# Normalising and storing the output rows inside the experts' block, with the rows of the later experts corrected afterwards

## The chip, the cores and the metric

The kernel runs on one core of one Trainium2 chip. The metric is the device time of one execution in microseconds (us), the median over several executions. Lower is better.

## What is computed

A decoder layer on 4 x 2048 tokens of 256 float32 values: attention with a layer norm, then a mixture of experts with a second layer norm. Only the second part is touched.

```python
logits = relu(x @ rw1 + rb1) @ rw2 + rb2
vals, ids = top_k(logits, 2)                     # two experts of eight for each token
probs = softmax(vals)
disp[e, pos] = x of the tokens sent to expert e  # at most 1024 rows for each expert
eo = relu(disp @ ew1 + eb1) @ ew2 + eb2
y = eo[ids, pos] * probs, summed over the two experts
out = layernorm(x + y)                           # over the 256 values of a row
```

So a row of the output needs the token's own x, the row of its first and the row of its second expert. Rows of one expert lie anywhere in the batch.

## The kernel before

The program has blocks with a barrier between them: projections, attention, `mix_and_route`, `experts`, `normalize`. `mix_and_route` writes x to the DRAM table `z_rows` and scatters every row, with three tags behind its 256 values (row number, rank, gap of the two logits), into `dispatched`.

**experts.** The rows of the 8 experts are worked in 16 halves of 512 rows (4 tiles of 128), named 0 to 15 here. Half 10 and 11 are those of expert 5, half 14 and 15 those of expert 7, the last. For each half TensorE (PE) runs `first` (8 groups of 6 matmuls, one group for each 128 of the 1024 hidden values), turns the next half's rows, and runs `second` (96 matmuls). Every product is made of three, with operands split into a high and a low float32r part. ScalarE (ACT) makes two ReLU copies of each group (L1867, L1870); VectorE (DVE) subtracts them (L1940) and signals `hid_done`. `first` waits for `hid_done` of the group four places back, since there are four banks; ACT's second copy waits for that of two groups back, since `hid` has two buffers. In even halves ACT and DVE also split the next expert's weights (L1844, L1847, L1887), which ends with the signal `weights_split`. DVE adds the bias (L1921), multiplies by the share (L1929), and GpSimd (POOL) issues four accumulating indirect DMAs for each half (L1776), which add 128 rows each into `z_rows`. After each odd half POOL waits until its adds have landed (`expert_added`). SP loads the rows of later halves, weights and biases.

**normalize.** After the barrier SP loads all of `z_rows` in 16 chunks of 512 rows; DVE makes the statistics and the scale of each row, ACT normalises three tiles of a chunk, POOL the fourth, and SP stores the chunk.

```python
            for ci in range(NCH):
                sp.dma_start(z[:, ci], z_src[ci]).then_inc(z_in[ci], 16)
            for ci in range(NCH):
                sp.wait_ge(act_result, MINE * (ci + 1))
                sp.wait_ge(pool_result, ci + 1)
                sp.dma_start(out_dst[ci], result[:, ci]).then_inc(stored, 16)
```

The order of every queue is written out by hand, in the order of the code.

Of the kernel before, what the change touches and what calls it, by code (L numbers as in the profile page):

```python
# [21 lines left out]
U32 = mybir.dt.uint32  # L22
# [20 lines left out]
TAGS = 3  # L43
ROW = C + TAGS
ROW_ID, FIRST, GAP = C, C + 1, C + 2
# [19 lines left out]
class Carried:  # L65
# [4 lines left out]
    def __init__(self, nc, ctx):  # L70
# [11 lines left out]
        self.rw1_in = s.sem("rw1_in")  # L82
# [726 lines left out]
def attend(nc, a, d, kept, first):  # L809
# [10 lines left out]
    with ExitStack() as ctx:  # L820
# [53 lines left out]
        def _(sp):  # L874
# [31 lines left out]
            def first_rows():  # L906

                for i in range(2):
                    sp.wait_ge(y_out[i], 16 * G * NC // 2)
                load_sums(sp, d, slice(0, EARLY), kept.sums[:], kept.sums_in[0])  # L910
                load_values(sp, d, 0, kept.yk, kept.rows_in[0])
                load_values(sp, d, 1, kept.yk1, kept.rows_in[1])
                sp.dma_start(kept.xr[:], x_src[0]).then_inc(kept.rows_in[0], 16)
                sp.dma_start(kept.rw1[:], a["rw1"].rearrange("(k p) n -> p k n", p=P)).then_inc(kept.rw1_in, 16)
# [141 lines left out]
        def _(pool):  # L1056
# [5 lines left out]
            nc.gpsimd.tensor_copy(empty_rows[:, :, ROW_ID].bitcast(U32), empty_ids[:]).then_inc(empty_set, 1)  # L1062
# [93 lines left out]
def mix_and_route(nc, a, d, kept, early):  # L1156
# [8 lines left out]
    with ExitStack() as ctx:  # L1165
# [20 lines left out]
        row_ids = sb("row_ids", [P, B * NC, TT])  # L1186
# [297 lines left out]
        def _(act):  # L1484
# [33 lines left out]
            ready(act, kept.rw1_in, 16)  # L1518
# [9 lines left out]
        def _(dve):  # L1528
# [84 lines left out]
            def place(c, n):  # L1613
# [18 lines left out]
                v.tensor_copy(tags[:, :, ROW_ID].bitcast(U32), row_ids[:, ci])  # L1632
# [62 lines left out]
def experts(nc, a, d, early):  # L1695


    HALVES = 2 * E
    RING = 4
    with ExitStack() as ctx:  # L1700
# [4 lines left out]
        rows = sb("rows", [P, RING, TT, ROW])  # L1705
        row_ids = sb("row_ids", [P, RING, TT], U32)
        is_first = sb("is_first", [P, RING, TT])
        other = sb("other", [P, RING, TT])
        ratio = sb("ratio", [P, RING, TT])
        total = sb("total", [P, RING, TT])  # L1710
        share = sb("share", [P, RING, TT])
# [10 lines left out]
        eo = sb("eo", [P, 2, TT, C])  # L1722
        xt_ps = [ps(f"xt{i}", [P, CH]) for i in range(KC)]
# [3 lines left out]
        rows_in = [sem(f"rows_in{i}") for i in range(RING)]  # L1727
        turned = sem("turned")
# [10 lines left out]
        expert_added = sem("expert_added")  # L1739
        share_step = sem("share_step")  # L1740
        other_done = sem("other_done")
        ratio_done = sem("ratio_done")
        share_done = sem("share_done")
        added = [sem(f"added{i}") for i in range(2)]
        block = ctx.enter_context(nc.Block())

        rows_src = d["disp"].rearrange("(h t p) c -> h p t c", p=P, t=TT)

        @block.sync
        def _(sp):  # L1750
            def load_rows(q):
                if q >= RING:
                    sp.wait_ge(turned, KC * (q - RING + 1))
                    sp.wait_ge(other_done, q - RING + 1)
                sp.dma_start(rows[:, q % RING], rows_src[q]).then_inc(rows_in[q % RING], 16)

            for q in range(RING):
                load_rows(q)
            for q in range(HALVES):
# [4 lines left out]
                if q + RING < HALVES:  # L1764
                    load_rows(q + RING)
                if q % 2 and e < E:
                    sp.wait_ge(eo_done, 2 * (q + 1))
                    early.load_biases(sp, e, e % SUBS)

        @block.gpsimd  # L1770
        def _(pool):
            for q in range(HALVES):
                pool.wait_ge(eo_weighed, TT * (q + 1))
                pool.sem_inc(early.due, 1)
                for t in range(TT):
                    pool.indirect_dma_start(  # L1776
                        d["z"], bass.IndirectOffsetOnAxis(ap=row_ids[:, q % RING, t:t + 1], axis=0),
                        eo[:, q % 2, t, :], None, compute_op=ALU.add,
                    ).then_inc(added[q % 2], 16)
                if q % 2:  # L1780
                    for i in range(2):
                        pool.wait_ge(added[i], 16 * TT * (q // 2 + 1))
                    pool.sem_inc(expert_added, 1)
# [54 lines left out]
        def _(act):  # L1838
# [16 lines left out]

            high_w1(0)
            rows_of(0)
            high_w2(0)
            for q in range(HALVES):
# [12 lines left out]
                act.wait_ge(other_done, q + 1)  # L1872
                nc.scalar.activation(ratio[:, q % RING], other[:, q % RING], ACT.Exp).then_inc(ratio_done, 1)
                if q + 1 < HALVES:
                    rows_of(q + 1)
                if q % 2 == 0 and q // 2 + 1 < E:
                    high_w1(q // 2 + 1)
                    high_w2(q // 2 + 1)

        @block.vector  # L1880
        def _(dve):
# [14 lines left out]
            def read_tags(q):  # L1896
                at = q % RING
                dve.wait_ge(rows_in[at], 16 * (q // RING + 1))
                if q >= RING:
                    dve.wait_ge(expert_added, q // 2 - 1)  # L1900
                nc.vector.tensor_copy(row_ids[:, at], rows[:, at, :, ROW_ID].bitcast(U32))
                nc.vector.tensor_scalar(is_first[:, at], rows[:, at, :, FIRST], rev[:, q // 2:q // 2 + 1], 2.0,
                                        ALU.is_equal, ALU.mult).then_inc(share_step, 1)
                dve.wait_ge(share_step, 2 * q + 1)
                nc.vector.scalar_tensor_tensor(other[:, at], is_first[:, at], -1.0, rows[:, at, :, GAP],
                                               ALU.add, ALU.mult).then_inc(other_done, 1)

            def weights_of(q):
                at = q % RING
                dve.wait_ge(ratio_done, q + 1)  # L1910
                nc.vector.tensor_scalar(total[:, at], ratio[:, at], 1.0, None, ALU.add).then_inc(share_step, 1)
                dve.wait_ge(share_step, 2 * q + 2)
                nc.vector.reciprocal(share[:, at], total[:, at]).then_inc(share_done, 1)

            def add_bias(q):
# [7 lines left out]
                dve.wait_ge(share_done, q + 1)  # L1923
                if q >= 2:
                    dve.wait_ge(expert_added, q // 2)
# [222 lines left out]
```

## Time and profile before

| | us |
|---|---|
| time, median of 3 executions (2829.73 to 2831.21) | 2830.01 |
| time of the profiled execution | 2830.7 |
| its span, from the first to the last instruction | 2828.7 |
| start of the experts' block | 2384.7 |
| start of `normalize` | 2781.8 |

The trace is that of one execution. A row of a timeline or of a group names engine, line, operation and the tiles read and written; an idle time in brackets has the instruction that ended it. Names that end in q (SPq, POOLq) are an engine's queue, with the instructions that only issue DMAs, wait or drain.

### The profile page before, as it was taken

The numbers are of one execution on the slowest core, as the hardware profiler recorded it, in microseconds if no ns is written. First come the engines' busy times: TensorE is split into PE (matmuls) and PEld (weight loads), VectorE is DVE, ScalarE is ACT, GpSimd is POOL, SyncE is SP. The second block draws the span as 40 slices with busy tenths as digits, with TensorE's granted clock in tenths as the row PEclk, the third lists the DMA queues.
The fourth block names the chain that finished last, engine by engine and source line by source line (L and its number), as shares of the span: only waits on it lengthen the run. The fifth ranks groups of instructions, "written<-read, shape, count | busy, mean of one in ns | idle before, by whom it ended". The sixth has DMA issues, their size and how long they took to land. (4 is left out here: it accounts for less than half of the span.)

```text
span 2828.7 us, 46886 instructions
## 1 busy us (share of the span) xinstructions
PE 2703.0 (96%) x16154; PEld 1869.5 (66%) x16154; DVE 2092.8 (74%) x5500; ACT 1785.7 (63%) x3322; POOL 760.1 (27%) x721
## 2 busy tenths in 40 slices
PE   8999989999999999999999999999899996999991
PEld 7888855666655656666665666566377774999991
DVE  7888879888888888888888888887355553545444
ACT  5666626677777677766777777777654444655554
POOL 7888820100100110110110010011025553222222
PEclk9999979999999999999999999999999997999995
DMA  6878863233442442532533333431074432343317
GB/s 218 281 266 281 283 171 87 65 99 94 105 106 77 98 98 61 132 83 75 119 82 91 85 91 85 104 91 51 12 222 150 127 105 80 76 103 84 72 23 245
DMA packets 241853, 337.91 MB, mean 119 GB/s; under 512 B 37986, under 2 KB 125195, under 8 KB 240336
## 3 DMA queue, kind: packets, MB, share of 16 engines
q1 hardware_dynamic: 223952, 311.72, 38.7%
q0 software_dynamic: 17664, 23.19, 4.1%
q8 instruction: 129, 2.11, 0.3%
q14 instruction: 108, 0.88, 0.1%
HBM read 191.47 MB, written 152.86 MB: 122 GB/s over the span
## 5 line engine op out<-in xcount | busy, mean ns | idle before, releaser
L1048 ACT ACTIVATE att_probs<-att_score_bank 128x512 f32<-128x512 f32 (+1 forms) x2240 | 1127.3, 596 | 460.6 <-PE att_score_bank L991 450.7
L1095 DVE TENSOR_REDUCE att_partial_max<-att_max_bank 128x1 f32<-128x512 f32 x1536 | 979.6, 682 | 173.0 <-PE att_max_bank L977 171.5
L991 PE MATMUL att_score_bank<-att_q_st,att_k_st 98*128 98x512 f32 (+3 forms) x1792 | 578.9, 381 | 7.8 <-DMA att_q_st<-att_max_rows 6.0
L977 PE MATMUL att_max_bank<-att_k_st,att_q_st 96*128 96x512 f32 (+3 forms) x1792 | 570.8, 374 | 1.7 <-DVE att_partial_max L1095 0.8
L1077 POOL TENSOR_SCALAR_AFFINE_SELECT att_probs<-att_probs 128x512 f32<-128x512 f32 x256 | 162.0, 635 | 1499.1 <-ACT att_probs L1048 1499.0
L1008 PE MATMUL att_acc_bank<-att_probs,att_v_st 128*32 128x512 f32 (+3 forms) x5120 | 528.2, 536 | 0.0
L1101 DVE CUSTOM_DVE_ANT_0 att_edge_sum<-att_max_bank,first_edge 128x256 f32<-128x256 f32 (+3 forms) x1024 | 459.5, 483 | 67.6 <-PE att_max_bank L977 65.6
L991 PEld LDWEIGHTS att_score_bank<-att_q_st,att_k_st 98*128 98x128 f32 x1792 | 319.8, 190 | 163.2 <-ACT att_probs L1048 80.6
L977 PEld LDWEIGHTS att_max_bank<-att_k_st,att_q_st 96*128 96x128 f32 x1792 | 330.2, 190 | 136.3 <-DVE att_partial_max L1095 53.1
L1008 PEld LDWEIGHTS att_acc_bank<-att_probs,att_v_st 128*32 128x32 f32 x5120 | 136.7, 109 | 248.8 <-issue 140.3
L289 POOL TENSOR_TENSOR proj_op_low<-proj_turned,proj_op_high 128x512 fp32r<-128x512 f32 x192 | 244.2, 1297 | 47.3 <-ACT proj_op_high L449 44.7
L1867 ACT ACTIVATE exp_hid_high<-exp_hid_bank,exp_b 128x512 fp32r<-128x512 f32 x128 | 88.3, 690 | 158.1 <-PE exp_hid_bank L1809 147.9
L1776 POOL DMA_INDIRECT z_rows<-exp_eo,exp_row_ids x64 | 108.4, 1694 | 287.6 <-DVE exp_eo L1929 241.7
L977 PE MATMUL att_max_bank<-first_k,att_q_st 96*128 96x512 f32 (+3 forms) x432 | 169.9, 415 | 6.1 <-DMA att_v_st<-v_tokens 5.6
L1509 ACT ACTIVATE mix_hid<-mix_hid_bank,mix_rb 128x512 f32<-128x512 f32 x128 | 87.7, 685 | 136.6 <-PE mix_hid_bank L1428 136.5
L1374 POOL DMA_INDIRECT dispatched<-mix_x,mix_scatter_idx x128 | 129.5, 1011 | 148.0 <-DVE mix_x L1634 112.3
L449 ACT ACTIVATE proj_op_high<-proj_turned 128x512 fp32r<-128x512 f32 x192 | 121.1, 631 | 68.8 <-DVE proj_turned L518 67.1
L1940 DVE TENSOR_TENSOR exp_hid_low<-exp_hid,exp_hid_high 128x512 fp32r<-128x512 f32 x128 | 88.6, 692 | 83.9 <-ACT exp_hid L1870 83.9
L991 PE MATMUL att_score_bank<-att_q_st,first_k 98*128 98x512 f32 (+3 forms) x432 | 150.6, 398 | 0.0
L1826 PE MATMUL exp_eo_bank<-exp_w_high,exp_hid_high 128*128 128x256 f32 x512 | 146.2, 286 | 0.0
L1826 PE MATMUL exp_eo_bank<-exp_w_high,exp_hid_low 128*128 128x256 f32 x512 | 145.0, 283 | 0.0
L1826 PE MATMUL exp_eo_bank<-exp_w_low,exp_hid_high 128*128 128x256 f32 x512 | 145.0, 283 | 0.0
(239 smaller groups left out, 4235.9 us busy)
## 6 DMA issues: line engine op xcount, KB each, us to landing
qk_parts<-proj_parts SPq DMA_DIRECT2D x64, 1024.0 KB, 5.2
att_k_st<-qk_parts SPq DMA_DIRECT2D x168, 256.0 KB, 6.5
att_q_st<-qk_parts SPq DMA_DIRECT2D x159, 256.0 KB, 4.5
v_tokens<-proj_v_tok SPq DMA_DIRECT2D x64, 256.0 KB, 4.6
att_v_st<-v_tokens SPq DMA_DIRECT2D x64, 256.0 KB, 7.2
y_heads<-kept_y_raw SPq DMA_DIRECT2D x64, 256.0 KB, 2.3
exp_w<-in_ew SPq DMA_DIRECT2D x16, 1024.0 KB, 8.7
first_q<-qk_parts SPq DMA_DIRECT2D x33, 256.0 KB, 4.4
```

Source lines behind the costliest of these rows:

```text
L289: nc.gpsimd.tensor_tensor(op_low[:, c % OPS, i], turned[:, c % 2, i], op_high[:, c % OPS, i].bitcast(F32), ALU.subtract).then_inc(lows_don ...
L449: nc.scalar.activation(op_high[:, c % OPS, i], turned[:, c % 2, i], ACT.Copy).then_inc(highs_done, 1)
L977: last = nc.tensor.matmul(max_ps[u % MAXB][:, at:end], q_tile(n)[0:3 * L, head, tile * P:(tile + 1) * P], k_tile(g, kb)[0:3 * L, head, 0:e ...
L991: last = nc.tensor.matmul(score_ps[h % SCOREB][:, i * (CH - q0):(i + 1) * (CH - q0)], k_tile(g, kt // TT)[:, j + i, (kt % TT) * P:(kt % TT ...
L1008: last = nc.tensor.matmul(acc[j * L:(j + 1) * L, q0:CH], v_st[:, g % 2, kt // TT, kt % TT, j * L:(j + 1) * L], probs[:, k % PROBS, j, q0:C ...
L1048: nc.scalar.activation(probs[:, k % PROBS, j:j + heads, q0:CH], score_ps[h % SCOREB][:, 0:heads * (CH - q0)].rearrange("p (j n) -> p j n", ...
L1077: nc.gpsimd.affine_select(out=block_probs, in_=block_probs, pattern=[[0, HG], [1, P]], compare_op=ALU.is_ge, fill=zero, base=0, channel_mu ...
L1095: nc.vector.tensor_reduce(partial_max[:, m % 2, j * TT + t, kb:kb + 1], bank[:], AX.X, ALU.max).then_inc(unit_reduced, 1)
L1101: last = nc.vector.tensor_tensor_reduce(out=edge_sum[:, u % 2, at:end], in0=bank[:, at:end], in1=edge[:, CH - end + at:CH], scale=1.0, sca ...
L1374: pool.indirect_dma_start(d["disp"], bass.IndirectOffsetOnAxis(ap=scatter_idx[:, c[1] % SUBS, kt:kt + 1], axis=0), x1[:, c[1] % ROUND, kt ...
L1776: pool.indirect_dma_start(d["z"], bass.IndirectOffsetOnAxis(ap=row_ids[:, q % RING, t:t + 1], axis=0), eo[:, q % 2, t, :], None, compute_o ...
L1826: last = nc.tensor.matmul(eo_ps[i][:, t, :], x[:, m, part], w[:, sub, m], start=(m == 0 and n == 0), stop=(m == MC - 1 and n == 2))
```

## The change

`normalize` is gone. Its work stands in the queues of `experts`, from half 10 on. It is done on units: c0 to c15 are chunks of 512 output rows, h10 to h15 the rows of one half.

- A chunk is loaded from `z_rows` when the adds of a given half have landed (`half_added`, now signalled after every half), normalised in place by ACT (three tiles) and POOL (one) and stored. c0 to c2 are loaded before half 10 is added, c3 to c5 before half 11, c6 to c8 before half 12, c9 and c10 before half 13, c11 to c15 after it.
- Rows that a later half changes are corrected: POOL gathers them by row number from `z_rows` (`gather`), ACT and DVE normalise two tiles each, and POOL scatters them into the output (`fix`), with a bound that leaves out rows whose chunk had not been stored yet.
- Expert 7's halves 14 and 15 are no longer added to `z_rows`. Their rows are gathered ahead, DVE adds the weighted result to them, and they are normalised and scattered directly.
- The statistics of a chunk or half are made either between the subtractions of half q (STATS_FIRST) or after them, ahead of the bias (STATS_SECOND).
- Every dispatched row has a fourth tag, its row in the output. The tags of all 16 halves are loaded once, by one DMA of 128 x 16 x 4 runs of 16 bytes, and all shares are computed once, in half 0; the DVE and ACT instructions that did it in each half (L1901 to L1913, L1873) are gone. Rows are loaded without tags, into a ring of 3 in place of 4.
- The DMA that loads `rw1` in attention counts on another semaphore, `consts_in`.

```diff
-TAGS = 3
+TAGS = 4
-ROW_ID, FIRST, GAP = C, C + 1, C + 2
+ROW_ID, FIRST, GAP = C, C + 2, C + 3
...
+HALVES = 2 * E
+LAST = HALVES - 2
+LOADED_IN = {10: (0, 1, 2), 11: (3, 4, 5), 12: (6, 7, 8), 13: (9, 10), 14: (11, 12, 13, 14, 15)}
+STATS_FIRST = {11: ("c1", "c2"), 12: ("c5",), 13: ("h10", "h11"), 14: ("c9", "c10"), 15: ("c13", "h12")}
+STATS_SECOND = {10: ("c0",), 11: ("c3", "c4"), 12: ("c6",), 13: ("c7", "c8"), 14: ("c11", "c12"), 15: ("h13", "c14", "c15")}
+def norms_in(q):
+    return STATS_SECOND.get(q - 1, ()) + STATS_FIRST.get(q, ())
...
-    RING = 4
+    RING = 3
+    SPARE = 5
...
 SP queue of experts, for each half q, between the loads of rows and of biases:
+                if q in LOADED_IN:
+                    sp.wait_ge(half_added, q)
+                    if q == 11:
+                        sp.wait_ge(weights_split, 2 * (E - 1))
+                    if q == 13:
+                        sp.wait_ge(weights_split, 2 * E)
+                    if q == LAST:
+                        sp.wait_ge(stored[0], 16 * 6)
+                    for i in LOADED_IN[q]:
+                        load_chunk(i)
...
+                if q > 10:
+                    for u in norms_in(q):
+                        if is_chunk(u):
+                            store_chunk(u)
...
 GpSimd queue of experts:
-            for q in range(HALVES):
-                pool.wait_ge(eo_weighed, TT * (q + 1))
...
+            def gather(q):
+                for t in range(TT):
+                    pool.indirect_dma_start(
+                        unit(f"h{q}")[:, t, :], None, d["z"],
+                        bass.IndirectOffsetOnAxis(ap=ids[:, q, t, 0:1], axis=0)).then_inc(gathered[max(q, 11)], 16)
+
+            def fix(q, group):
+                pool.wait_ge(act_result, results(f"h{q}", TT - 1, 2))
+                pool.wait_ge(dve_result, results(f"h{q}", 0, 2))
                 pool.sem_inc(early.due, 1)
                 for t in range(TT):
                     pool.indirect_dma_start(
-                        d["z"], bass.IndirectOffsetOnAxis(ap=row_ids[:, q % RING, t:t + 1], axis=0),
+                        out_rows, bass.IndirectOffsetOnAxis(ap=ids[:, q, t, 1:2], axis=0),
+                        unit(f"h{q}")[:, t, :], None, bounds_check=bounds[group], oob_is_err=False,
+                    ).then_inc(fixed[group], 16)
+
+            def add(q):
+                pool.wait_ge(eo_weighed, TT * (q + 1))
+                for i in LOADED_IN.get(q, ()):
+                    pool.wait_ge(*loaded_at[i])
+                if q == 12:
+                    pool.wait_ge(gathered[11], 16 * 2 * TT)
...
+                pool.wait_ge(added, 16 * TT * (q + 1))
+                pool.sem_inc(half_added, 1)
+
+            for q in range(LAST - 1):
+                add(q)
+                if q == 11:
+                    pool.wait_ge(weights_split, 2 * E)
+                    gather(10)
+                    gather(11)
+                if q == 12:
+                    pool.wait_ge(stored[0], 16 * 6)
+                    fix(10, 0)
+                    fix(11, 0)
+                for u in norms_in(q + 1):
+                    if q + 1 > 10 and is_chunk(u):
+                        norm_chunk(u)
+            add(LAST - 1)
+            gather(LAST)
+            pool.wait_ge(fixed[0], 16 * 2 * TT)
+            gather(12)
+            for u in norms_in(LAST):
+                if is_chunk(u):
+                    norm_chunk(u)
+            gather(13)
+            gather(LAST + 1)
+            for u in norms_in(HALVES - 1):
+                if is_chunk(u):
+                    norm_chunk(u)
+            pool.wait_ge(stored[1], 16 * 5)
+            fix(12, 1)
+            norm_chunk("c14")
+            norm_chunk("c15")
+            fix(13, 1)
+            pool.wait_ge(stored[2], 16 * 5)
+            pool.wait_ge(fixed[1], 16 * 2 * TT)
+            fix(LAST, 2)
+            fix(LAST + 1, 2)
+            pool.wait_ge(fixed[2], 16 * 2 * TT)
...
 ScalarE queue of experts, after the eight ReLU pairs of half q:
+                if q == 0:
+                    act.wait_ge(share_step, 4)
+                    nc.scalar.activation(ratio[:], other[:], ACT.Exp).then_inc(ratio_done, 1)
+                if q > 10:
+                    for u in norms_in(q):
+                        deviation(u)
                 if q + 1 < HALVES:
                     rows_of(q + 1)
...
+                if q in range(11, HALVES - 1):
+                    for u in sorted(norms_in(q), key=is_chunk):
+                        norm(u)
+            norm("h12")
+            deviation("h13")
+            norm("h13")
+            for u in ("c11", "c12", "c13"):
+                norm(u)
+            for u in ("c14", "c15", "h14", "h15"):
+                deviation(u)
+                norm(u)
...
 VectorE queue of experts:
+            def arrived(u):
+                if is_chunk(u):
+                    dve.wait_ge(*loaded_at[number(u)])
+                elif number(u) < LAST:
+                    dve.wait_ge(gathered[max(number(u), 11)], 16 * TT * (2 if number(u) < 12 else 1))
...
                 for m in range(MC):
                     dve.wait_ge(hid_high_done, MC * q + m + 1)
                     nc.vector.tensor_tensor(hid_low[:, m], hid[:, m % 2], hid_high[:, m].bitcast(F32),
                                             ALU.subtract).then_inc(hid_done, 1)
+                    if m < len(tiles):
+                        stats_of(*tiles[m])
+                        if m:
+                            moments_of(*tiles[m - 1])
...
+            all_moments("h13")
+            all_moments("c14")
+            finish_half("h13")
+            all_moments("c15")
+            scales_of("c14")
+            all_moments("h14")
+            scales_of("c15")
+            finish_half("h14")
+            add_bias(HALVES - 1)
+            all_moments("h15")
+            finish_half("h15")
-def normalize(nc, d, out):
...
```

## Rows read from the trace of the kernel before

**Rows 1.** The page, part 1: engine, busy us (share of the span), instructions.

```profile
PE 2703.0 (96%) x16154; PEld 1869.5 (66%) x16154; DVE 2092.8 (74%) x5500; ACT 1785.7 (63%) x3322; POOL 760.1 (27%) x721
```

**Rows 2.** Stretches: PE, PEld, DVE, ACT, POOL busy, granted clock, DMA share, GB/s.

```profile
2698.30:2721.70 23.40, 23.40 (x154) 21.42 (x154) 9.90 (x23) 11.22 (x20) 6.81 (x4) 1.00 0.20 24
...
2782.00:2828.70 46.70, 0.00 (x0) 0.00 (x0) 29.62 (x160) 30.65 (x65) 8.87 (x16) 0.50 0.98 360
```

**Rows 3.** Timeline 2762 to 2800: start us, us, engine, line, operation, [idle before].

```profile
2765.96 0.69 DVE L1921 TENSOR_TENSOR exp_eo_sum<-exp_eo_bank,exp_b 128x512 f32<-128x512 f32 x1 [5.07 <-PE exp_eo_bank L1826]
...
2774.74 1.55 POOL L1776 DMA_INDIRECT z_rows<-exp_eo,exp_row_ids  x1 [0.31 <-issue]
2781.78 9.43 SPq L1997 DMA_DIRECT2D fin_z<-z_rows  x16
...
2785.04 1.41 DVE L2028 BATCH_NORM_STATS2 fin_stats<-fin_z 128x6 f32<-128x256 f32 x4 [17.35 <-DMA fin_z<-z_rows]
```

**Rows 4.** Issues of the final stores, L2001: ns min/median/max, first and last start.

```profile
L2001 SPq DMA_DIRECT2D out<-fin_result x16: 792/1336/5053, 2791.3 to 2820.7; - x16
```

**Rows 5.** SP and POOL at block ends (L1700 experts', L1959 normalize's).

```profile
L1700 POOLq DRAIN  x1: 2982/2982/2982, 2778.6 to 2778.6; - x1
...
L1959 POOLq DRAIN  x1: 691/691/691, 2815.5 to 2815.5; - x1
```

**Rows 6.** Indirect DMAs by line: ns min/median/max; then issue to landing, us.

```profile
L1374 POOL DMA_INDIRECT dispatched<-mix_x,mix_scatter_idx x128: 978/981/1509, 2097.8 to 2379.3; - x128
...
DMA to landing us min/median/max: 2.1/2.5/5.0
```

**Rows 7.** The same for the accumulating scatters of the experts.

```profile
L1776 POOL DMA_INDIRECT z_rows<-exp_eo,exp_row_ids x64: 1539/1557/2023, 2419.9 to 2774.7; - x64
...
DMA to landing us min/median/max: 3.6/4.1/8.6
```

**Rows 8.** POOL timeline, the first two adds of half 12.

```profile
2699.45 1.55 POOL L1776 DMA_INDIRECT z_rows<-exp_eo,exp_row_ids  x1 [15.58 <-DVE exp_eo L1929]
2701.30 1.79 POOL L1776 DMA_INDIRECT z_rows<-exp_eo,exp_row_ids  x1 [0.30 <-issue]
```

**Rows 9.** ACT timeline, turned rows in half 12, start of half 13.

```profile
2685.80 1.08 ACT L1854 ACTIVATE exp_rows_high<-exp_xt_bank 128x512 fp32r<-128x512 f32 x2
...
2698.32 0.69 ACT L1867 ACTIVATE exp_hid_high<-exp_hid_bank,exp_b 128x512 fp32r<-128x512 f32 x1 [7.84 <-PE exp_hid_bank L1809]
```

**Rows 10.** DVE timeline, halves 12 and 13.

```profile
2685.84 0.69 DVE L1940 TENSOR_TENSOR exp_hid_low<-exp_hid,exp_hid_high 128x512 fp32r<-128x512 f32 x1 [0.67 <-ACT exp_hid L1870]
...
2688.71 4.49 DVE L1887 TENSOR_TENSOR exp_w_low<-exp_w,exp_w_high 128x2048 fp32r<-128x2048 f32 x2 [0.98 <-ACT exp_w_high L1844]
...
2697.54 1.13 DVE L1929 TENSOR_SCALAR exp_eo<-exp_eo_sum,exp_share 128x256 f32<-128x256 f32 x4
```

**Rows 11.** PE timeline: half 12 begins; its second layer begins after the turning.

```profile
2673.43 0.40 PE L1809 MATMUL exp_hid_bank<-exp_rows_high,exp_w_high 128*128 128x512 f32 x1
...
2685.14 0.36 PE L1826 MATMUL exp_eo_bank<-exp_w_high,exp_hid_high 128*128 128x256 f32 x1
```

**Rows 12.** Groups by line from 2350: count | busy us, mean ns | idle before.

```profile
L2013 ACT ACTIVATE fin_result<-fin_z,fin_shift,fin_rstd 128x256 f32<-128x256 f32 x48 | 25.2, 590 | 0.2 <-DVE fin_shift L2037 0.2
L2028 DVE BATCH_NORM_STATS2 fin_stats<-fin_z 128x6 f32<-128x256 f32 x64 | 22.3, 411 | 17.3 <-DMA fin_z<-z_rows 17.3
...
L1991 POOL TENSOR_SCALAR fin_result<-fin_z,fin_rstd,fin_shift 128x256 f32<-128x256 f32 x16 | 8.9, 554 | 25.4 <-DVE fin_shift L2037 25.2
```

**Rows 13.** DMA issues, whole kernel: KB each, median us to landing.

```profile
exp_rows<-dispatched SPq DMA_DIRECT2D x16, 518.0 KB, 5.3
...
mix_rw<-in_rw SPq DMA_DIRECT2D x1, 32.0 KB, 3.5
```

**Rows 14.** PE's waits, longest first; granted clock around the second.

```profile
PE att_score_bank L991 <- DMA att_q_st<-att_max_rows: 6.0, 1, 6.0
...
2008.00:2014.00 6.00, 3.86 (x8) 0.50 0.39 120
```

More of the change, by code:

```diff
@@ L1692, in load_first, with is_chunk, number, results @@
             self.load_biases(sp, sub, sub)
-def experts(nc, a, d, early):
-    HALVES = 2 * E
-    RING = 4
+HALVES = 2 * E
[3 more added lines that the diff above has]
+STATS_SECOND = {10: ("c0",), 11: ("c3", "c4"), 12: ("c6",), 13: ("c7", "c8"), 14: ("c11", "c12"), 15: ("h13", "c14", "c15")}
+UNITS = [u for q in range(10, HALVES) for u in STATS_FIRST.get(q, ()) + STATS_SECOND[q]] + ["h14", "h15"]
+AT = {u: i for i, u in enumerate(UNITS)}
+def norms_in(q):
+    return STATS_SECOND.get(q - 1, ()) + STATS_FIRST.get(q, ())
+NORMED = [u for q in range(11, HALVES - 1) for u in sorted(norms_in(q), key=lambda u: u[0] == "c")]
+NORMED += ["h12", "h13", "c11", "c12", "c13", "c14", "c15", "h14", "h15"]
+def is_chunk(u):
+    return u[0] == "c"
+def number(u):
+    return int(u[1:])
+def results(u, of_chunk, of_half):
+    return sum(of_chunk if is_chunk(v) else of_half for v in NORMED[:NORMED.index(u) + 1])
+STORED_IN = ((0, 6), (6, 11), (11, 16))
+def experts(nc, a, d, early, out):
+    RING = 3
+    SPARE = 5
     with ExitStack() as ctx:
@@ new lines, in experts @@
+        z_in = {}
+        gathered = {q: sem(f"gathered{q}") for q in range(11, HALVES)}
+        stats_done = sem("stats_done")
+        moments_done = sem("moments_done")
+        std_done = sem("std_done")
+        rstd_done = sem("rstd_done")
+        norm_ready = sem("norm_ready")
+        act_result = sem("act_result")
+        pool_result = sem("pool_result")
+        dve_result = sem("dve_result")
+        stored = [sem(f"stored{i}") for i in range(len(STORED_IN))]
+        fixed = [sem(f"fixed{i}") for i in range(3)]
@@ L1749, in _, with unit @@
+        loaded_at = {}
+        for i in range(B * NC):
+            place = homes[f"c{i}"][0]
+            if place not in home_in:
+                home_in[place] = sem(f"in_{place}")
+            loaded_at[i] = home_in[place], 16 * (1 + sum(homes[f"c{k}"][0] == place for k in range(i)))
+        def unit(u):
+            return homes[u][1]
         @block.sync
@@ L1932, in _, with norm, finish_half @@
+            def norm(u):
+                at = AT[u]
+                dve.wait_ge(norm_ready, at + 1)
+                for t in range(2, TT):
+                    nc.vector.tensor_scalar(unit(u)[:, t], unit(u)[:, t], rstd[:, at, t:t + 1], shift[:, at, t:t + 1],
+                                            ALU.mult, ALU.add).then_inc(dve_result, 1)
+            def finish_half(u):
+                scales_of(u)
+                norm(u)
             dve.wait_ge(ident_in, 32)
@@ L1936, in _ @@
             for q in range(HALVES):
-                read_tags(q)
+                tiles = [(u, t) for u in STATS_FIRST.get(q, ()) for t in range(TT)]
                 for m in range(MC):
@@ L2058, in const_arrays @@
     row = np.arange(P)
+    chunk, tile = np.arange(B * NC)[None, :, None], np.arange(TT)
     return {
@@ L2061, in const_arrays @@
         "rev": np.tile(E - np.arange(E, dtype=f), (P, 1)),
-        "row_ids": ((np.arange(B * NC)[None, :, None] * P + row[:, None, None]) * TT + np.arange(TT)).astype(f),
+        "row_ids": np.stack([(chunk * P + row[:, None, None]) * TT + tile, (chunk * TT + tile) * P + row[:, None, None]], axis=-1).astype(f),
         "empty_ids": (N + row[:, None] * 8 + np.arange(8)).astype(f),
@@ L2129, in program @@
         kept_ctx.close()
-        experts(nc, a, d, early)
-    normalize(nc, d, out)
+        experts(nc, a, d, early, out)
 def kernel(**inputs):
```

275 lines of the change are left out of this document (146 added, 129 removed).

## The prediction

> **What bounds the kernel now.** I read the page first: PE is busy for 96% of the span [rows 1], so what can be won lies where PE has nothing to do. The stretches show where [rows 2]: in half 13 PE is busy throughout, DVE 9.9 and ACT 11.2 of 23.4 us, POOL 6.8. After 2782.0 PE does nothing, and the DMA engines are busy for 98% of the 46.7 us. The timeline shows the hand-over [rows 3]: PE's last sum is taken at 2765.96, the last add is issued at 2774.74, the chunks are asked for at 2781.78, and the first statistics start at 2785.04. Between them POOL drains for 2.98 us before the barrier opens [rows 5]. The last store is issued at 2820.7 [rows 4]. So 2828.7 - 2766.0 = 62.7 us lie behind PE's last product, and the change is about them. Inside the experts' block the period of a half is (2699.45 - 2419.9) / 12 = 23.3 us [rows 7, 8], and PE sets it.
>
> **The start of the block.** The tags come as 128 x 16 x 4 = 8192 runs of 16 bytes. The nearest row is rw2's load, 1024 runs of 32 bytes, landed after 3.5 us [rows 13]; eight times that is 28 us with the fixed part counted eight times, and with a fixed part of about 2 us (the fastest landing in rows 6) it is 2 + 8 x 1.5 = 14 us. Issued near 2386.5, the tags are in at 2400. DVE asks for them after half 0's eight subtractions, near 2407, and the turned rows that then wait for ACT and DVE (about 4 us, with the Exp behind its table load) are needed by PE near 2417. So the load is free up to some 26 us. The other end goes by the rows' load, 512 runs of 1036 bytes in 5.3 us [rows 13]: 16 x (5.3 - 2) + 2 = 55 us, a stall of 29 us. I take nothing, as the runs of 32 bytes are nearer in size. The Trainium skill (DMA: Bandwidth & Descriptors, Specifications) puts the least size for line rate at 512 bytes; the 3.5 us for 32-byte runs agree that a run, not a byte, is what is paid for.
>
> The rest of the start is small: a row of 1040 bytes for 1036, one cast of 8 tags for 4, a ring of three whose loads are still asked for a half or more ahead of a landing of 5.3 us. The instructions on tags and shares in each half go, under PE's cover, and count as nothing. One landing wait for each half in place of each expert is hidden too: four adds at 1.70 + 0.30 us and 4.1 to land end some 11 us into a half of 23.3 [rows 7, 8]. One ACT table load moves from the end into half 11, and is covered by ACT's idle half.
>
> **Halves 10 to 12.** DVE's statistics of a chunk tile are 0.41 us (0.33 in a row) [rows 12]. Between two subtractions DVE is idle for 0.67 us [rows 10], so one tile with its small aggregate, some 0.45 us, fits. ACT normalises a chunk in three steps of about 0.5 us, POOL in one of 0.55 [rows 12]; three or four chunks in a half are at most 6.2 us on ACT against 12 idle. No cost. But ACT makes three deviations before half 12's turned rows, and the last waits for DVE's last subtraction (2685.84 + 0.69): the turned rows start at 2687.0, not 2685.80 [rows 9]. The split of the last weights behind them ends 1.2 us later, at 2688.71 + 4.49 + 1.2 = 2694.4 [rows 10].
>
> **Half 13: a new stall.** POOL's gathers of halves 10 and 11 go into the raw weights' place and wait for that split. No row shows a gather. I take the plain indirect scatter, 0.98 + 0.30 us apart, landing 2.5 us after its issue [rows 6]; the upper bound is the accumulating one, 1.70 + 0.30 and 4.1 [rows 7, 8]. It lies nearer to the plain one, since it moves 128 rows one way and adds nothing. The eighth is issued at 2694.4 + 7 x 1.28 = 2703.4 and lands at 2705.9. DVE waits for all eight right behind its first subtraction of half 13, in front of the second. That one then ends at 2705.9 + 0.35 + 0.69 = 2707.0. PE's sixth group needs it. Half 13 starts on PE at 2673.43 + 23.3 = 2696.7 [rows 11], a group takes 1.36 (0.69 + 0.67 [rows 10]), so it was due at 2703.5. **Stall: 3.5 us**, and ACT and DVE catch up inside the 11.7 us [rows 11] up to the second layer. At the accumulating price it is 7 x 0.72 + 1.6 = 6.6 us more.
>
> **POOL's queue after it.** It now holds, besides the adds, 24 gathers and 24 fixes, each 1.28 us. In order:
> - add 12: behind eight gathers and three chunk tiles at 2706.5, and 0.8 for the start of an indirect DMA after a wait (2697.54 + 1.13 to 2699.45 [rows 8, 10]): 2707.3, where it was 2699.45. Landed at 2707.3 + 6.0 + 4.1 = 2717.4.
> - fixes 10 and 11: 2718.2 to 2729.1. One tile, and add 13 starts at 2730.5. It was due at 2722.8 + 3.5 = 2726.3, so POOL is 4 us behind. Landed at 2740.6.
> - gathers 14 and 12, four tiles, gathers 13 and 15, three tiles: 16 x 1.28 + 7 x 0.6 = 24.7, so 2765.5. Half 14's rows are in near 2747, a little before DVE wants them; half 15's near 2766.
> - fix 12 up to 2771.3. Then c14 and c15, whose scales come late: ACT has c11 to c13 before their deviations, and DVE holds h14's statistics behind them. POOL has c15 at 2774.6.
> - fix 13 from 2775.9; its rows must have landed before fix 14: 3 x 1.28 + 2.5, so 2782.3.
> - fix 14 from 2783.0, fix 15 from 2788.8, the last issue at 2792.6, landed at 2795.1.
> - POOL's drain, 2.98 after indirect DMAs, where `normalize` ended with one of 0.69 [rows 5]: the span ends at 2798.4.
>
> PE itself ends at 2766.0 + 3.5 = 2769.5. The values of h15 would be ready at about 2782.5: DVE comes to its bias near 2777.5, behind c14, c15 and h14, and needs about 5 us for bias, sum, statistics and scale. So POOL's queue, not PE, sets the end, by 6 us.
>
> **Sum.** Out: 62.7 us behind PE's last product. In: 3.5 of stall and 28.9 from PE's end to the last drain. Net -30.3 us, on a profiled time of 2830.7, which is 0.7 above the median of the runs shown. From the median it gives 2799.7, so 2800.
>
> **Rivals.**
> - *The stall of half 13 is larger.* With gathers at 1.6 us the eight take 5 us more, and with the other sixteen the queue ends 12 us later: 2812. Or the clock falls: a wait of 6.0 us in attention had a granted clock of 0.50 (1.2 GHz) around it, with 8 matmuls in 6 us [rows 14]. A stall of 3.5 us may do the same; if ten us then ran at half speed, they would cost 5 more: 2805. Against it, the wait is shorter. Range 2804 to 2814.
> - *POOL is quicker than its row.* Fixes leave rows out by their bound, and gathers may cost less. Then the ACT and DVE chain of the end decides: 2782.5, four fixes, landing and drain, 2782.5 + 0.7 + 3.8 + 2.5 + 3.3 = 2792.8 in the span, a time of 2794.
> - *The other side: POOL's plain indirect DMAs are dearer.* All 48 lie in one queue that sets the end, two thirds of the way without slack. At 1.55 us each instead of 0.98 the same walk gives an end some 23 us later, 2823. The walk loses about 41 us for each us of price (of the 48, some seven lie in slack), so from 0.98 + 30.3 / 41 = 1.72 us each on, the kernel isn't faster; at 1.92 it is slower, 2838. For it: the add beside DVE's work takes 1.79 where it otherwise takes 1.55 [rows 8]. Against it: 128 plain scatters beside DVE's work in `mix_and_route` have a median of 0.98 [rows 6]. The Trainium skill (SBUF — State Buffer, Who interferes with whom) says that a DVE instruction in a two-port mode keeps GpSimd from writing descriptors for its whole length; by that rule the new DVE work would lengthen POOL's issues. The 1.79 may be that, and the 0.98 doesn't show it.
> - *The tags' load stalls half 0.* It decides from 26 us on; at the 55 us above 29 us are lost and the time is 2829, about the same as before.
>
> **How the numbers follow.** Forecast 0.60, with its own range of 2795 to 2806; a larger stall 0.18; quicker POOL 0.10; dearer POOL 0.09, of which 0.04 slower than before, 0.02 the same and 0.03 faster; tags 0.03, of which 0.01 faster, 0.01 same and 0.01 slower. A range of 2792 to 2816 holds the first three and part of the fourth. About 0.2% (5.7 us) is what a measurement can tell from no change. Faster: 0.60 + 0.18 + 0.10 + 0.03 + 0.01 = 0.92; same 0.03; slower 0.05.
>
> **What the new profile would show.** Right: PE waits once for 3 to 4 us in half 13, for DVE's subtraction; DVE's wait before it is ended by the gathers; plain gathers and fixes about 1 us each on POOL; PE's last product near 2769; POOL without long gaps from 2730 to the end, and its drain last in the chain. Wrong: PE waiting in halves 0 or 1 for turned rows (tags), or in half 14 or 15 for a bias or subtraction; gathers of 1.5 us; the last chain on ACT and DVE; a clock of 0.5 after the stall.

## The result and the profile after

The kernel after takes 2808.89 us (median of four runs, 2802.61 to 2810.47), the kernel before 2829.87 beside it: a ratio of 0.9925, with an interval of 0.9905 to 0.9945. Run once more beside a later experiment it took 2805.84 against 2830.13 (0.9912, 0.9897 to 0.9928). Two executions in a slow state, of 4361 us (that later run) and of 5291 us (experiment 2), are left out. Ratios, here and below, are estimates of their own and differ by up to 0.0005 from the quotient of the two medians. The prediction said 2800 and faster; the direction is right, the gain is 21 to 24 us and not 30. The first median lies outside the range that it gave its own forecast, 2795 to 2806, and inside that of its rival of a larger stall, 2804 to 2814; the second lies in both. The profiled execution has a span of 2808.7 us, where the prediction's sum ended at 2798.4. These 10.3 us are what has to be found.

The page, part 1, of the kernel after:

```profile
PE 2708.5 (96%) x16154; PEld 1871.6 (67%) x16154; DVE 2105.0 (75%) x5498; ACT 1791.4 (64%) x3325; POOL 796.5 (28%) x761
```

Against [rows 1] POOL has 40 instructions and 36 us more; PE's busy time rose by 5.5 us although it does the same matmuls: some ran slowly.

The tags' load in the page's DMA issues (KB, us to landing):

```profile
exp_tags<-dispatched SPq DMA_DIRECT2D x1, 128.0 KB, 10.1
```

The gathers by their line (ns min/median/max, first and last start; then issue to landing), and the scatters that put rows right by theirs:

```profile
L1886 POOL DMA_INDIRECT exp_w<-z_rows,exp_ids x16: 947/951/1448, 2697.5 to 2763.2; - x16
...
DMA to landing us min/median/max: 2.7/3.1/7.3
```

```profile
L1895 POOL DMA_INDIRECT out<-exp_w,exp_ids x16: 982/988/1286, 2724.3 to 2787.6; - x16
```

The unknown prices were well bounded: 0.95 us a gather, 0.98 to 0.99 a scatter, as [rows 6] had it. The tags were in after 10.1 us, before DVE asked.

What PE waited for in the last four halves (total, times, longest):

```profile
PE exp_hid_bank L1982 <- DVE exp_hid_low L2193: 5.1, 2, 4.0
```

Three stretches of half 13 (PE, PEld, DVE, ACT, POOL busy, granted clock, DMA share, GB/s):

```profile
2700.00:2712.00 12.00, 8.02 (x33) 6.33 (x32) 4.82 (x14) 5.82 (x10) 9.31 (x10) 0.92 0.48 147
2712.00:2716.00 4.00, 4.00 (x11) 3.03 (x11) 3.08 (x10) 1.78 (x3) 3.35 (x3) 0.50 1.06 242
2716.00:2724.00 8.00, 8.00 (x60) 7.57 (x59) 5.78 (x21) 6.35 (x14) 1.56 (x1) 0.95 0.66 168
```

The wait in half 13 is 4.0 us. Around its end the granted clock falls to 0.50, the level of 1.2 GHz, for 12 x 0.08 + 4 x 0.50 + 8 x 0.05 = 3.4 us of lost clock, that is 6.8 us at half. Part of these PE still stood idle: its 14 matmuls from 2710.69 to 2716.83 would have taken 3.2 us at the 0.23 us of those ahead of the wait and took 6.1, so some 3.0 us more. The other wait, 1.1 us, is in half 15. In front of each stands DVE, waiting for rows; from its timeline:

```profile
2709.62 0.43 DVE L2153 BATCH_NORM_STATS2 exp_stats<-exp_w 128x6 f32<-128x256 f32 x1 [6.31 <-DMA exp_w<-z_rows,exp_ids]
...
2757.60 1.92 DVE L2136 SCALAR_TENSOR_TENSOR exp_eo<-exp_eo_sum,exp_share,exp_eo 128x256 f32<-128x256 f32 x4 [3.24 <-DMA exp_eo<-z_rows,exp_ids]
```

Rows of POOL's timeline: the first of half 12's additions, of half 10's scatters and of half 13's additions, the tiles of chunks 14 and 15, the first of half 14's scatters, and the last scatter:

```profile
2710.51 1.64 POOL L1915 DMA_INDIRECT z_rows<-exp_eo,exp_ids  x1 [0.96 <-DMA exp_w<-z_rows,exp_ids]
...
2724.25 1.04 POOL L1895 DMA_INDIRECT out<-exp_w,exp_ids  x1 [6.43 <-DVE exp_w L2178]
...
2735.72 1.61 POOL L1915 DMA_INDIRECT z_rows<-exp_eo,exp_ids  x1 [0.17 <-issue]
...
2780.79 0.55 POOL L1904 TENSOR_SCALAR exp_spare<-exp_spare,exp_rstd,exp_shift 128x256 f32<-128x256 f32 x1 [3.82 <-DVE exp_shift L2171]
2783.00 0.56 POOL L1904 TENSOR_SCALAR exp_spare<-exp_spare,exp_rstd,exp_shift 128x256 f32<-128x256 f32 x1 [1.65 <-DVE exp_shift L2171]
...
2790.61 0.98 POOL L1895 DMA_INDIRECT out<-exp_eo,exp_ids  x1 [1.90 <-DMA out<-exp_w,exp_ids]
...
2799.62 0.98 POOL L1895 DMA_INDIRECT out<-exp_eo,exp_ids  x1 [0.30 <-issue]
```

And the drain behind it, by the block's line:

```profile
L1736 POOLq DRAIN  x1: 6257/6257/6257, 2802.2 to 2802.2; - x1
```

It takes 6.26 us where the kernel before had 2.98 [rows 5]. The last scatter goes out at 2799.62 where the sum had 2792.6, and 7.0 + 3.3 = 10.3: the whole miss. Of the 7.0, 2.4 were there when the block began (its first transposition starts at 2391.0, before at 2388.6). So the questions are the 2.4, the 4.6 inside POOL's queue, and the 3.3 of drain.

Since the start of the block moves between executions, I compare two lengths in each trace: from the block's first transposition to the start of its last product on PE (377.0 us before, 386.1 after), and to POOL's last scatter (forecast 2792.6 - 2388.6 = 404.0; measured 408.6, and 407.8 in the second profile).

### The profile page after: what moved, and what is told of

It is laid out like the page before. It is cut to its first block and busy times, and to the rows that moved or that the text cites. A ratio compares the mean times of both kernels' runs of the same rounds, so it can differ in the third digit from the quotient of the medians.

```text
span 2808.7 us, 46944 instructions
## 1 busy us (share of the span) xinstructions
PE 2708.5 (96%) x16154; PEld 1871.6 (67%) x16154; DVE 2105.0 (75%) x5498; ACT 1791.4 (64%) x3325; POOL 796.5 (28%) x761
## 5 line engine op out<-in xcount | busy, mean ns | idle before, releaser
L1915 POOL DMA_INDIRECT z_rows<-exp_eo,exp_ids x56 | 94.8, 1693 | 215.2 <-DVE exp_eo L2133 201.3
```

## The experiments

**1. Half 10's gathers counted alone.** So that DVE in half 13 waits for four gathers and not eight (half 12's gathers, which come much later, count on from there; POOL waits for both halves' before half 12's additions):

```diff
-.then_inc(gathered[max(q, 11)], 16)
+.then_inc(gathered[12 if q == 10 else q], 16)
...
-dve.wait_ge(gathered[max(number(u), 11)], 16 * TT * (2 if number(u) < 12 else 1))
+dve.wait_ge(gathered[12 if u == "h10" else number(u)], 16 * TT * (2 if u == "h12" else 1))
```

> The kernel after, with one change: the gathers of half 10 count on a semaphore of their own, so that VectorE in half 13 waits for the four gathers of half 10 alone (the fourth landed about 5 us before the eighth) and needs those of half 11 four statistics later. Theory A (the 8.5 us by which TensorE's last product comes late beyond the shift of the block are the wait for the eighth gather, 4.0 us, and the slow matmuls at clock 0.50 that it brings on, 3.4 us): the wait in half 13 is under 1 us, no stretch at 0.50 there, PE's last product 7 us earlier against the start of the block. The time falls by less than that, since POOL's queue sets the end: its last scatters wait for norms that wait for PE, so 3 to 5 us, about 2804 to 2806. Theory B (the clock falls there in any case, because of the drop in load around half 12 to 13): the wait goes, 0.50 stays, PE 4 us earlier, time 2806 to 2807. Theory C (POOL's own issues alone set the end): PE earlier, time within 1 us of the kernel after.

2804.9 us (0.991, 0.9894 to 0.9925). The wait and the slow stretch of half 13 are gone. Both are back later: DVE now waits behind its subtractions of half 14, and PE, for the subtraction that stands behind this, in the first layer of half 15. DVE's timeline, then PE's, then two stretches of this kernel:

```profile
2744.60 1.41 DVE L2154 BATCH_NORM_STATS2 exp_stats<-exp_spare 128x6 f32<-128x256 f32 x4 [8.04 <-DMA exp_spare<-z_rows]
```

```profile
2754.76 0.79 PE L1983 MATMUL exp_hid_bank<-exp_rows_high,exp_w_high 128*128 128x512 f32 x1 [5.26 <-DVE exp_hid_low L2194]
```

```profile
2748.00:2754.00 6.00, 1.49 (x7) 0.91 (x5) 5.32 (x14) 0.77 (x2) 5.18 (x8) 0.88 0.95 346
2754.00:2760.00 6.00, 5.24 (x14) 4.15 (x15) 5.02 (x15) 3.19 (x6) 4.74 (x5) 0.55 1.04 341
```

DVE comes to chunk 11 earlier, but chunk 11 is loaded once half 13's additions have landed, and POOL issues these behind eight scatters. PE's length is 385.9 us, POOL's 408.2: nothing won. Theory B fell (the clock stays at 1.00 in half 13 when the wait goes), and so did A's 7 us on PE and 3 to 5 in the time; C isn't tested, since PE wasn't earlier at its end. The lower median, though inside A's 2804 to 2806, doesn't settle it, for the two medians of the kernel after lie 3 us apart and in the profiled executions the blocks began at 2388.0 and 2391.0; the lengths, which leave the start out, are what speaks against a gain. The wait was not half 13's own: it belonged to POOL's queue.

**2. The upstream edits alone** (fourth tag, ids, router weights' semaphore) in the kernel before.

```diff
-TAGS = 3
+TAGS = 4
...
-row_ids = sb("row_ids", [P, B * NC, TT])
+row_ids = sb("row_ids", [P, B * NC, TT, 2])
...
-ready(act, kept.rw1_in, 16)
+ready(act, kept.consts_in, 48)
```

> The kernel before, with nothing but what the change does ahead of the experts' block: a fourth tag per row (rows of 1040 in place of 1036 bytes), the table of row ids twice as large, and the router weights' load counted on another semaphore. Theory A (the 2.4 us by which the experts' block starts later belong to these edits): the block starts 2 to 3 us later than in the kernel before, the mix block's stretch 2096 to 2119 shows the longer waits, time 2831 to 2833. Theory B (it is jitter between executions, or comes from elsewhere): the block starts within 0.7 us of before and the time is within 1 us of before.

2829.4 us, ratio 0.9999 (0.9990 to 1.0008). The edits by themselves cost nothing that can be measured, though the interval leaves room for 2 to 3 us. In the six profiles of the kernel before and its variants the first transposition starts between 2383.2 and 2388.6, in the eight of the kernel after and its variants between 2384.7 and 2391.0; the means are 2385.9 and 2388.3, and the ranges overlap. So the 2.4 us of the first pair of profiles are no more than what one execution differs from the next; whether a part of them is the change's stays open.

**3, 4, 8, 11. POOL's drain.** Four variants of the kernel before: one gather; a bound on the additions; eight gathers on one semaphore; the additions on four semaphores in place of two. The edit of the third (the eighth has eight gathers in its loop), then of the fourth, then of the eleventh:

```diff
+if q == 11:
+    pool.indirect_dma_start(probe[:], None, d["z"],
+        bass.IndirectOffsetOnAxis(ap=row_ids[:, q % RING, 0:1], axis=0)).then_inc(probed, 16)
+    pool.wait_ge(probed, 16)
...
-    eo[:, q % 2, t, :], None, compute_op=ALU.add,
+    eo[:, q % 2, t, :], None, compute_op=ALU.add, bounds_check=bound, oob_is_err=False,
...
-    ).then_inc(added[q % 2], 16)
+    ).then_inc(added[q % 4], 16)
```

> The kernel before, with one gather (row ids of half 11, from the rows in DRAM into a tile that nothing reads) issued by POOL once half 11 is added, and waited for. Looked at for POOL's drain at the end of the experts' block, 2.98 us before and 6.26 us in the kernel after. Theory A (a gather in the block adds the 3.3 us): drain about 6.2. Theory B (it grows with the count of indirect DMAs, 64 against 104, 0.08 us each): drain about 3.1. Theory C (the bounded plain scatters do it): about 3.0 here.

> The kernel before, with a bound (never exceeded) on the 64 accumulating scatters of the experts' block. Looked at for POOL's drain at the end of that block and for the price of an issue. Theory C of the drain (bounded scatters add the 3.3 us): drain about 6.2, and the issue stays 1.54 to 1.56 us. Theories A and B: drain about 3.0.

> The kernel before, with eight gathers in place of the third experiment's one, all on one semaphore. Looked at for POOL's drain at the end of the experts' block (2.98 us before, 3.35 us with one gather, 6.26 us in the kernel after). Theory A (0.37 us per gather): 5.9 us. Theory B (0.37 us for one more semaphore that indirect DMAs count on): 3.35 us. Theory C (by the count of indirect DMAs in the block, 0.08 us each): 3.6 us.

> The kernel before, with the additions counted on four semaphores in place of two, and nothing else. Looked at for POOL's drain at the end of the experts' block. Theory A (a part of the drain goes by the number of semaphores on which indirect DMAs count, 0.33 us each, as one gather on a new one against eight gathers on it suggests): 3.6 us. Theory B (it goes by the work alone): 2.98 us.

The drain's rows in the third, eighth and eleventh, in this order:

```profile
L1700 POOLq DRAIN  x1: 3350/3350/3350, 2776.7 to 2776.7; - x1
```

```profile
L1700 POOLq DRAIN  x1: 3636/3636/3636, 2773.3 to 2773.3; - x1
```

```profile
L1700 POOLq DRAIN  x1: 3309/3309/3309, 2775.9 to 2775.9; - x1
```

In the fourth it is 2.982 us, as before, and an addition's issue 1.556. So a bound costs nothing; seven more gathers cost 3.636 - 3.350 = 0.286 us, 0.041 each; two more semaphores cost 3.309 - 2.982 = 0.327. No theory holds alone. The kernel after has 104 indirect DMAs against 64 (24 of them gathers), and nine semaphores that they count on against two: 40 x 0.041 + 7 x 0.164 = 2.8 of the 3.28 us, if scatters count as gathers do. That is an estimate, and two things on record speak against it as a rule. By it the third run's one gather on one new semaphore would cost 0.2 us, and it cost 3.350 - 2.982 = 0.37. And `mix_and_route`, in the kernel before, issues 128 scatters on four semaphores and drains in 2.669 us, less than the 64 additions on two: scatters don't seem to count:

```profile
L1165 POOLq DRAIN  x1: 2669/2669/2669, 2381.8 to 2381.8; - x1
```

Without them it is 24 x 0.041 + 7 x 0.164 = 2.1 us. So 1.2 of the 3.28 us, or at best 0.5, stay open.

**5. POOL scatters half 11 behind half 13's additions and half 14's gathers**, on top of experiment 1:

```diff
                     fix(10, 0)
-                    fix(11, 0)
...
             gather(LAST)
+            fix(11, 0)
             pool.wait_ge(fixed[0], 16 * 2 * TT)
```

> The kernel of the first experiment (gathers of half 10 counted alone), with one more change: POOL stores the put-right rows of half 11 behind the additions of half 13 and the gathers of half 14, no longer ahead of them. Theory A (POOL's queue is what the block waits for: in the first experiment VectorE stood 8.0 us for chunk 11 in half 14, which is loaded when the additions of half 13 have landed, and these stood behind 8 scatters of 1.3 us): the additions go out about 5.5 us earlier, the wait for chunk 11 falls to 2 to 3 us, TensorE's wait of 5.3 us and the stretch at clock 0.55 in half 14 go, PE's last product comes 7 us earlier against the start of the block, and the time is 2799 to 2802. Theory B (the wait moves on once more, to the gathers of half 14 or to rows of half 12): TensorE has a wait of over 3 us later in halves 14 or 15, and the time is 2803 to 2806.

2802.31 us (0.9907, 0.9892 to 0.9922). PE's only wait in the last four halves is now this one, and the clock is 1.00 up to PE's end:

```profile
PE exp_eo_bank L2000 <- DVE exp_hid_low L2194: 0.4, 1, 0.4
```

Two stretches of its half 15, where experiment 1 had its stall:

```profile
2748.00:2754.00 6.00, 5.73 (x35) 4.83 (x33) 4.10 (x14) 4.68 (x10) 5.27 (x7) 1.00 0.70 225
2754.00:2760.00 6.00, 5.89 (x49) 5.89 (x50) 2.32 (x14) 1.40 (x3) 4.47 (x6) 1.00 0.89 284
```

PE's length is 378.4 us, 7.7 less than in the kernel after; POOL's is 405.0, 3.6 less (2.8 against the second profile). Theory A's mechanism holds, and its time (2799 to 2802) but for 0.3 us. It also gives the rate of exchange: of 7.7 us won on PE some 3 to 4 arrive at the end.

**6. The end's order alone**, in the kernel after: ScalarE takes the deviations early, and POOL scatters half 13 ahead of the last two tiles.

```diff
             deviation("h13")
+            deviation("c14")
             norm("h13")
-            for u in ("c11", "c12", "c13"):
-                norm(u)
-            for u in ("c14", "c15", "h14", "h15"):
-                deviation(u)
-                norm(u)
+            norm("c11")
+            deviation("c15")
+            norm("c12")
+            norm("c13")
+            deviation("h14")
...
             fix(12, 1)
+            fix(13, 1)
             norm_chunk("c14")
             norm_chunk("c15")
-            fix(13, 1)
```

> The kernel after, with the order of the last ten microseconds alone changed: ScalarE takes the deviations of chunks 14 and 15 as soon as their moments are there (ahead of norms of half 13 and chunk 12), that of half 14 ahead of the norms of chunk 14, and POOL scatters half 13 before it norms the last tiles of chunks 14 and 15. Theory A (the end of the queue waits 3.8 and 1.7 us for scales that stand behind nine norms on ScalarE): POOL's waits for DVE shrink to under 1 us, the first scatter of half 14 goes out about 3 us earlier, time 2805 to 2807. Theory B (the wait for the stores of chunks 14 and 15, 1.9 us in the kernel after, takes it back, since these now stand behind four scatters): time within 1 us of the kernel after, with a wait of 4 us or more for the stores ahead of half 14's scatters.

2805.03 us (0.9916, 0.9902 to 0.9929). POOL's length is 407.2, against 408.6 and 407.8. The waits for the scales (3.8 and 1.7 us in the kernel after) are gone, and the next one took their place:

```profile
2784.66 0.99 POOL L1895 DMA_INDIRECT out<-exp_eo,exp_ids  x1 [5.12 <-DMA out<-exp_spare]
```

The time is in theory A's range, and the first scatter of half 14 goes out 1.4 us earlier in the block (398.2 against 399.6), where A had 3. Theory B's mechanism is what the trace shows: the stores of chunks 14 and 15 now stand behind the scatters.

**7. Experiments 5 and 6 together.**

> The fifth and sixth experiments together: half 10's gathers counted alone, half 11 scattered behind half 13's additions, and the new order at the end. Theory A (two separate limits, TensorE's stall and the order at the end): both gains add, about 7 to 8 us under the kernel of the first experiment, 2796 to 2799. Theory B (with TensorE earlier, POOL's own issues are gapless to the end and set it alone): no more than 2 us under the fifth experiment.

2804.14 us (0.9910, 0.9895 to 0.9925), POOL's length 404.2: 0.8 under experiment 5. The wait for the stores is 4.7 us. The gains don't add, as theory B said, but the queue isn't gapless, so its reason misses as well as A; that the wait for the stores is now the limit is read from the trace.

**9. Experiment 5 with ScalarE's new order only**, POOL's old one.

> The fifth experiment with ScalarE's new order of the sixth, but POOL's old order at the end (tiles of chunks 14 and 15 ahead of half 13's scatters). Theory A (in the fifth experiment POOL still stood 2.4 and 1.7 us for the scales of chunks 14 and 15; it was only the scatters put ahead of these tiles that brought on the 4.7 us for the stores in the seventh): POOL's waits for DVE are under 1 us, no wait for a store, and from the block's first transposition to POOL's last scatter it takes 401 to 402 us, against 405.0 in the fifth experiment and 404.2 in the seventh; time 2798 to 2800. Theory B (half 13's own norms now come later and hold POOL as long): 404 us or more.

2801.37 us (0.9903, 0.9888 to 0.9918), POOL's length 404.0: 1.0 less than in experiment 5, not the 3 to 4 expected. The waits for scales are gone, and half 13's scatters start at 2770.47; behind them stands a new wait. Its row in POOL's timeline, then three stretches ahead of it:

```profile
2780.84 0.98 POOL L1895 DMA_INDIRECT out<-exp_eo,exp_ids  x1 [5.09 <-DMA out<-exp_w,exp_ids]
```

```profile
2766.00:2770.00 4.00, 0.00 (x0) 0.00 (x0) 3.39 (x20) 4.00 (x10) 3.37 (x5) 0.90 0.53 178
2770.00:2775.00 5.00, 0.00 (x0) 0.00 (x0) 4.06 (x11) 4.76 (x11) 3.92 (x5) 0.50 1.00 326
2775.00:2780.00 5.00, 0.00 (x0) 0.00 (x0) 2.46 (x12) 1.39 (x3) 0.75 (x1) 0.50 0.70 225
```

The last scatter of half 13 is issued at 2774.77 and lands 5.28 us later, in the kernel after 2.2. Here the DMA engines are busy for 1.00 of the stretch ahead of it and 0.70 of the next, with the five stores of chunks 11 to 15; in the kernel after it was 0.16 from 2788 to 2790, while that scatter landed. That the stores are what delays the landing is argued from these rows; no run left them out.

**10. The kernel after again**, beside experiment 9.

> The kernel after once more, unchanged, to have its time beside the ninth experiment on the same chip. Theory A (the 2.4 us by which the block began late in the profiled execution of the kernel after are jitter): the block's first transposition starts within 2385 to 2391, as it did in the other executions, and the time is 2806 to 2809. Theory B (they belong to the change): it starts at 2391 again.

2805.84 us (0.9912, 0.9897 to 0.9928), so experiment 9 is 4.5 us under it. The block began at 2390.3: inside theory A's range and 0.7 us from theory B's 2391, so it doesn't part them.

**12. Fewer semaphores for POOL to wait on**, on top of experiment 9: the loads of a half count on one semaphore, and POOL waits on four of them in place of eleven.

```diff
-for i in LOADED_IN.get(q, ()):
-    pool.wait_ge(*loaded_at[i])
+if q in LOADED_IN:
+    pool.wait_ge(*loaded_at[LOADED_IN[q][0]])
```

> The ninth experiment, with the loads of chunks 0 to 10 counted on one semaphore for each of the four halves in which they are issued, so that POOL waits on 4 semaphores for them in place of 11. VectorE then waits for the last load of its half's two or three. Theory A (POOL's drain grows by 0.16 us for each semaphore on which POOL waits in the block: two more gave 0.33 us in the eleventh experiment, and the first experiment, with one more, 0.16 us over the kernel after): the drain is 6.42 - 7 x 0.1635 = 5.28 us, the block about 1 us shorter, time about 2800. Theory B (the drain grows with the indirect DMAs alone, or with the semaphores that they count on, and these are as before): 6.42 us, time unchanged.

2804.4 us (0.9912, 0.9898 to 0.9925), POOL's length 404.3.

```profile
L1736 POOLq DRAIN  x1: 6420/6420/6420, 2796.7 to 2796.7; - x1
```

The drain is what it was in experiment 9, to the nanosecond. Theory A fell: POOL's waits for loads don't enter the drain.

## Why the prediction came out as it did

- **What bounds the kernel; removed 62.7 us:** right. Behind PE's last product nothing but the last chunks' norms, the rows of halves 12 to 15 and the drain are left, 31.3 us (2808.7 - 2777.4) in place of 62.7.
- **Start of the block, tags:** right. Expected to take some 14 us, it took 10.1; DVE took them at 2409.85, and no wait followed. The rule that the prediction cites from the Trainium skill (DMA: Bandwidth & Descriptors, Specifications), that short runs miss line rate, agrees: 128 KB in 10.1 us is 13 GB/s. The other bound, 55 us, was far off.
- **Price of gathers and scatters:** right, 0.95 and 0.98 us. The rule on GpSimd and two-port instructions from the Trainium skill (SBUF — State Buffer, Who interferes with whom) would have made them dearer beside DVE's new work; the medians don't show it, and single ones of 1.29 to 1.45 us may be it.
- **"Stall: 3.5 us":** its place and cause were right (4.0 us in half 13, DVE behind the gathers), its size was not. This term should have read 8.1: 4.0 of wait, 3.0 of matmuls at clock 0.50 after it, which the prediction had as a rival, and 1.1 in half 15, which it had not. There the gathers of half 14 landed 7.3 us after their issue, beside five loads of 512 KB. Of the wait itself the sum missed little: the first gather goes out 306.5 us after the first transposition where it had 305.8, for it left out the 0.8 us from a wait to an indirect DMA that it counts elsewhere. Experiment 5 removes wait, slow clock and second wait together, 7.7 us. Two of the prediction's signs of being wrong came with them: a clock of 0.50 after the stall, and PE waiting in half 15 for a subtraction.
- **"POOL's queue, not PE, sets the end":** right in the main. Experiment 1 took half 13's wait away and won nothing; experiment 5 took 7.7 us off PE and won 3 to 4. So the larger stall alone doesn't explain the time, and that the first median lies in that rival's range is partly luck: it priced the stall itself, while the end came late by POOL's queue and its drain.
- **The walk through the queue:** 4.6 us short from first transposition to last scatter. Fix 10 went out 3.6 us later than in the sum. POOL stood 6.4 us there; 3.3 of these are half 12's landing, which the sum had, and the other 3.1 DVE's norms of half 10, which came late with the stall (in experiment 1, without the stall in half 13, POOL stands there 3.3 us). Chunk 15's tile is then done 6.5 us late, since the scales of chunks 14 and 15 waited for ScalarE, the first behind nine norms, for longer than the sum had (POOL stood 3.8 and 1.7 us); about 2 us come back, because the sum left room behind that tile and at the landing. Two of its steps hold more than their prices give: 2718.2 + 8 x 1.28 is 2728.4, not 2729.1, and half 13's scatters start 1.3 us behind chunk 15's tile with no more than 0.7 to pay for it. In experiment 9, without either wait, the length is 404.0 us as forecast. That agreement is in part chance: fix 11 stands elsewhere in its queue, and a wait of 5.1 us for a landing has come in.
- **"POOL's drain, 2.98":** the step that failed without a rival. It measured 6.26. The row of before was carried over as if a drain had one price, but it differs from program to program. Gathers and semaphores account for 2.1 us of the 3.28, by the estimate above; the cause of the rest stays open.
- **The block's start:** 2.4 us of the 10.3; a sum against one profiled execution can't hold them, whichever they are.

So 2.4 + 4.6 + 3.3 = 10.3. Counted from the first transposition to the span's end, 440.1 us became 417.7: 22.4 are won, of the 30.3 that the sum had, and 4.6 + 3.3 are the difference.

## What to carry over

When a wait is found on one engine, ask which queue feeds it before moving the wait: taken away in half 13 (4.0 us on PE), it came back in half 15 (5.3 us), since both were POOL's queue seen from DVE. An engine that issues every indirect DMA is a queue with an order; put what others wait for ahead of what nobody waits for. And a price read from a block's end, such as a drain, belongs to that block's program: here it was 2.98 us before and 6.26 after.

## What the runs showed of the hardware

POOL's drain at the end of the experts' block was the same to the nanosecond in both profiles of the kernel after, and in variants that only move work: 6.257 us in these two and experiment 6, 6.420 in the five that count half 10's gathers apart, though the block began anywhere from 2384.7 to 2391.0. Between programs it differs: in variants of the kernel before by 0.041 us for each gather more, by 0.16 for each semaphore more that the additions count on, and by nothing for a bound; in experiment 12 by nothing for fewer waits on loads. In the kernel after a wait of 4.0 us on PE came with a granted clock of 0.50 for 6.8 us; in experiment 1 one of 5.3 us came with 0.55 in the stretch from 2754 to 2760; around the 1.1 us of the kernel after the clock stayed at 1.00.
